# Convolution attention's score products from 16-bit halves instead of 32-bit operands, on one Trainium2 core

## The reference

```
k, v, q = conv1x1(x, wk, bk), conv1x1(x, wv, bv), conv1x1(x, wq, bq)   # (4, 128, 1024) each
attn    = softmax(einsum('bcn,bcm->bnm', v, q), axis=2)                # (4, 1024, 1024)
av      = einsum('bcn,bnm->bcm', k, attn)                              # (4, 128, 1024)
x       = relu(bn2(conv1x1(bn1(wwg @ av), wout, bout)) + x)
t       = tokens(x);  t = t + attention_8_heads(layernorm(t));  t = t + moe_8_experts_top2(layernorm(t))
```

## Time and profile before

| | |
|---|---|
| Three runs, median | 1309.75 us (1306.08 to 1310.2) |
| Profiled execution, its own time | 1310.52 us |
| Its span, first to last instruction | 1308.7 us (1.8 us lie around it) |
| TensorE busy | 88% of the span |
| VectorE busy | 61% |
| ScalarE busy | 48% |
| GpSimd busy | 44% |
| Mean granted TensorE clock | 0.936 of full speed |

### The profile page before, as it was taken

How to read it: one execution, slowest core, us unless ns; L and a number is a source line. 1 busy time by engine, 2 the same in 40 slices (tenths; PEclk the granted TensorE clock), 3 DMA queues, 4 the chain that set the end, 5 groups by cost and what they waited for, 6 DMA issues and landing times. The chain is left out here.

```text
span 1308.7 us, 29280 instructions
## 1 busy us (share of the span) xinstructions
PE 1151.3 (88%) x10343; PEld 759.2 (58%) x10343; DVE 792.5 (61%) x1425; ACT 630.8 (48%) x1129; POOL 577.6 (44%) x455
## 2 busy tenths in 40 slices
PE   3999799996589999999999998159999999999993
PEld 2555454644334444445445444049999999998772
DVE  2546545565578878778877871735565556555540
ACT  0636356464257756775776675223333333333332
POOL 1314224241358865276257526434444444444330
PEclk9989899896679999999999999569999999999996
DMA  4126652443412323232142413712333323332227
GB/s 125 50 65 208 272 168 88 139 144 110 129 41 55 79 77 73 73 97 90 43 110 78 106 43 100 269 34 41 49 50 49 51 49 50 49 50 43 41 32 263
DMA packets 99246, 120.47 MB, mean 92 GB/s; under 512 B 29400, under 2 KB 76440, under 8 KB 98488
## 3 DMA queue, kind: packets, MB, share of 16 engines
q1 hardware_dynamic: 78152, 70.29, 18.3%
q0 software_dynamic: 20544, 42.22, 14.5%
q10 hardware_dynamic: 432, 6.29, 1.2%
HBM read 72.97 MB, written 45.60 MB: 91 GB/s over the span
## 5 line engine op out<-in xcount | busy, mean ns | idle before, releaser
L823 ACT ACTIVATE WB<-PP 128x512 f32<-128x512 f32 x512 | 268.5, 606 | 167.5 <-PE PP L1132 167.4
L1449 DVE TENSOR_REDUCE mxp<-PP 128x2 f32<-128x1024 f32 x256 | 301.3, 1218 | 66.4 <-PE PP L1065 65.1
L868 ACT ACTIVATE WORK<-PP,b1c 128x256 f32<-128x256 f32 (+1 forms) x320 | 143.5, 449 | 258.4 <-PE PP L896 254.8
L633 POOL TENSOR_TENSOR WB<-WB 128x1024 f32<-128x1024 f32 x80 | 188.6, 2358 | 79.5 <-PE PP L1121 71.3
L896 PE MATMUL PP<-WORK,WB 128*128 128x256 f16 (+1 forms) x1920 | 207.9, 264 | 3.2 <-DVE WORK L1750 3.1
L1244 PE MATMUL PP<-WB,WORK 128*128 x1704 | 193.8, 273 | 0.0
L896 PEld LDWEIGHTS PP<-WORK,WB 128*128 x1920 | 176.6, 99 | 29.6 <-issue 4.2
L1244 PEld LDWEIGHTS PP<-WB,WORK 128*128 128x128 f16 x1704 | 164.4, 98 | 20.9 <-issue 0.4
L1132 PE MATMUL PP<-WORK 97*128 97x256 f16 x1024 | 160.6, 281 | 8.5 <-ACT WB L823 5.4
L601 POOL TENSOR_TENSOR WB<-WORK,WB 128x1024 f16<-128x1024 f32 x32 | 68.1, 2129 | 218.4 <-ACT WORK L734 218.4
L697 POOL DMA_INDIRECT res_d<-WORK,lb x71 | 115.7, 1630 | 102.8 <-DVE WORK L1777 87.5
(11 more groups left out here) (255 smaller groups left out, 1169.4 us busy)
## 6 DMA issues: line engine op xcount, KB each, us to landing
WORK<-in_L_ffn_W_dram POOLq DMA_DIRECT2D x32, 512.0 KB, 4.3
res_d<-WORK SPq DMA_DIRECT2D x8, 1024.0 KB, 4.5
late_d<-WB POOLq DMA_DIRECT2D x1, 6144.0 KB, 18.7
WB<-late_d ACTq DMA_DIRECT2D x3, 2048.0 KB, 17.8
WORK<-in_x_dram SPq DMA_DIRECT2D x8, 512.0 KB, 3.8
v_d<-WORK SPq DMA_DIRECT2D x4, 1024.0 KB, 4.8
WORK<-q_hi_d SPq DMA_DIRECT2D x16, 256.0 KB, 3.9
WORK<-v_d SPq DMA_DIRECT2D x8, 512.0 KB, 5.6
```

Of the source, the lines that this page charges most:

```text
L633: pool.tensor_tensor(PS[n % 2], PR[n % 3][:, 0], PR[n % 3][:, 1], ALU.add).then_inc(s("pair_kept"), 1)
L823: act.activation(PR[n % 3][:, c // 2, c % 2 * 2:c % 2 * 2 + 2], SCORES[m % 3] .rearrange("p (h n) -> p h n", h=2), ACT.Exp).then_inc(s("e_ ...
L868: act.activation(hid[u][:, k, 0:width], hidden_bank(k)[:, 0:width], ACT.Gelu, bias=b1c[:, bass.ds(e, 1), k], scale=1.0 / WSCALE)\
L1449: dve.tensor_reduce(mxp[:, n // 4 % 2, i, h:h + 2, k], PP[2 + h // 2][:, :].rearrange("p (h n) -> p h n", h=2), X_AXIS, ALU.max).then_inc( ...
```

## The change

Queries and values of the convolution attention are no longer kept as f32. Each is kept as two f16 tensors in the same bytes: the value rounded to f16 (index 0), and what that rounding left, again in f16 (index 1). ScalarE writes the first (same instruction, f16 output). VectorE writes the second in one new instruction each for q and v, `low_halves`: PSUM plus bias minus the first half. It stands at the head of `keep_k`, so ahead of the write of k on VectorE. Each score product of 512 columns becomes three f16 matmuls summed in the same bank: lead with lead, lead of v with rest of q, rest of v with lead of q. The product of the two rests is left out. TensorE waits for `q_low` and `v_low` in place of `q_kept` and `v_kept`, in both places. Two semaphore names that nothing used make room for the new two.

```
-        q_sb, v_sb = QV[:, 0:N], QV[:, N:2 * N]
+        qc, vc = [QV[:, i * N:(i + 1) * N].bitcast(F16).rearrange("p (s n) -> p s n", s=2) for i in range(2)]
...
             def keep_q(n):
                 act.wait_ge(s("q_made"), n + 1)
-                act.activation(q_sb, PP[0][:, :], ACT.Identity, bias=vec[:, BQ:BQ + 1]).then_inc(s("q_kept"), 1)
+                act.activation(qc[:, 0], PP[0][:, :], ACT.Identity, bias=vec[:, BQ:BQ + 1]).then_inc(s("q_kept"), 1)
...
             def keep_v(n):
                 act.wait_ge(s("v_made"), n + 1)
-                act.activation(v_sb, PP[1][:, :], ACT.Identity, bias=vec[:, BV:BV + 1]).then_inc(s("v_kept"), 1)
+                act.activation(vc[:, 0], PP[1][:, :], ACT.Identity, bias=vec[:, BV:BV + 1]).then_inc(s("v_kept"), 1)
...
                 def scores(i):
                     if i == 0:
-                        pe.wait_ge(s("q_kept"), b + 1)
-                        pe.wait_ge(s("v_kept"), b + 1)
+                        pe.wait_ge(s("q_low"), b + 1)
+                        pe.wait_ge(s("v_low"), b + 1)
...
                     for h in range(2):
                         product(PP[i % 3][:, h * HALF:(h + 1) * HALF],
-                                [(v_sb[:, i * P:(i + 1) * P], q_sb[:, h * HALF:(h + 1) * HALF])],
+                                [(vc[:, sv, i * P:(i + 1) * P], qc[:, sq, h * HALF:(h + 1) * HALF])
+                                 for sv, sq in ((0, 0), (0, 1), (1, 0))],
                                 "sc_made" if h else None)
...
                 if not last:
                     project_x(b + 1, False)
-                    pe.wait_ge(s("q_kept"), b + 2)
-                    pe.wait_ge(s("v_kept"), b + 2)
+                    pe.wait_ge(s("q_low"), b + 2)
+                    pe.wait_ge(s("v_low"), b + 2)
...
+            def low_halves(n):
+                for made, to, at, name in ((PP[0], qc, BQ, "q"), (PP[1], vc, BV, "v")):
+                    dve.wait_ge(s(f"{name}_kept"), n + 1)
+                    dve.scalar_tensor_tensor(out=to[:, 1], in0=made[:, :], scalar=vec[:, at:at + 1], in1=to[:, 0],
+                                             op0=ALU.add, op1=ALU.subtract).then_inc(s(f"{name}_low"), 1)
+
             def keep_k(n):
+                low_halves(n)
                 dve.wait_ge(s("k_made"), n + 1)
```

More of the change, by code:

```diff
@@ L297, in s @@
             return S[name]
-        for name in ("ld_w ld_x0 ld_x1 x_used pool_const pe_prep dve_prep act_prep mv_prep "
+        for name in ("ld_w ld_x0 ld_x1 x_used pool_const pe_prep dve_prep act_prep q_low "
                      "q_made v_made k_made q_kept v_kept k_kept sc_made max_kept exp_kept ks_kept "
@@ L303, in hybrid_block @@
                      "vt_kept_a vt_kept_v res0_kept st_res0 st_v st_q0 st_q1 "
-                     "ld_stage0 ld_stage1 scaled split_hi split_lo st_last wts_split "
+                     "ld_stage0 ld_stage1 v_low split_hi split_lo st_last wts_split "
                      "ld_g0 ld_g1 ld_m0 ld_m1 sum_kept rin_kept rstd_kept ld_nm mx_made mx_kept pair_kept ld_sum inv_kept st_inv ld_inv0 ld_inv1 st_made e_kept pv_made nrm_kept "
```

## The result

The changed kernel took 1293.62 us (median of 4 runs, 1290.95 to 1294.65) against 1309.28 us for the kernel before (4 runs, 1306.08 to 1310.2): ratio 0.9879, 95% interval 0.9866 to 0.9893, so 15.7 us less.

The account below looks back on a forecast made before the run. TensorE was taken to bound the score loops: 13.5 us from the products, less 1.2 (scores 3), 1.4 (keys 6) and 0.3 (store), gives 10.6, so 1309.75 becomes 1299 us. Range 1294 to 1305.

Parts of the forecast that it names:

- The products: Score loops on TensorE: three f16 matmuls at 0.216 us replace 0.86 us of f32, saving 13.5 us in all.
- The wait before scores 3: Head of the score loop: TensorE waits for exponential 0 on ScalarE, since they share a bank; 0.3 us lost a pass.
- The collision on keys 6: Score loop: VectorE's scaling for tile 6 waits out a GpSimd instruction, delaying weigh 6 by 0 to 0.7 us a pass; 0.35 taken.
- The rests: Two more VectorE instructions a pass, before k, lie in idle time with 1.0 us in hand; cost taken 0.
- The store: Pass 1: a 6 MB store delays the next image's x load; up to 0.3 us of the gain stays behind.
- another chain in the loop: Rival: in the score loop late keys 6 or the staging ring take over from TensorE; 1302 to 1305, chance 0.13.
- uncovered rests: Rival: VectorE's rests run slower or start late before the transposes; up to 5.1 us lost, 1304, chance 0.06.
- no effect: Rival: in the score products, f16 records at 0.29 us make three as dear as two f32 ones; 1309, chance 0.05.
- a slower run: Rival: granted clock falls in the score loops; a third of each at the lower level gives 1330, chance 0.05.
- overlapping matmuls: Rival: a score bank's three products overlap wholly and the ring bounds the loop; 6 us less a pass, 1286, chance 0.01.
- The clock dip: Score loops: granted clock falls, work takes twice its time; gain gone from 3 us of such work a pass, chance 0.05.
- The sustained figure of 131 ns: Skill's pace for 512-column matmuls in a stream; would put a product at 0.39 us and the products' gain at 30 us.

Follow-up runs that it names:

- e3: Changed kernel with a fourth product, rest with rest, for each score bank: 1313.2 us against 1316.53 for the kernel before, 0.9981.
- e9: Kernel before with the fourth weight part moved out of the score loop, after exponential 7: 1313.11 us against 1309.18 for the kernel before, 1.0022.
- e2: Kernel before, f32 products kept, plus the two VectorE rest instructions a pass and TensorE's waits on them: 1315.42 us against 1316.53, 0.9991.
- e8: Changed kernel with v's rest made three times before TensorE is told: 1302.74 us against 1309.18 for the kernel before, 0.9947.
- e10: Changed kernel with the 6 MB store cut in three 2 MB stores started earlier: 1289.61 us against 1310.39 for the kernel before, 0.9834.
- e11: Kernel before with the 6 MB store cut in the same three 2 MB stores: 1302.24 us against 1310.39 for the kernel before, 0.9937.
- e4: Changed kernel with two products for each score bank, without the queries' rests: 1299.77 us against 1316.53 for the kernel before, 0.9877.
- e6: Changed kernel with one product for each score bank, lead by lead: 1290.32 us against 1310.39 for the kernel before, 0.9852.
- the other three sets: Changed kernel, no edit, run again three times against the kernel before: ratios 0.9908, 0.9873 and 0.9885.
- e1: Changed kernel run again, no edit: 1304.2 us against 1316.53 for the kernel before, 0.9908.

## Why the prediction was wrong in size

- **The products**: right. 0.216 us a matmul was measured, 0.42 us a tile, 13.5 us, and e3 shows that inside the loop nothing but the pace counts.
- **The wait before scores 3**: mis-sized. 0.3 us a pass was taken off. The four tiles of scores 0 to 3 take 189.19 - 183.87 = 5.32 us for 24 matmuls at 0.216, 5.18 us, so 0.14 are lost, all of it before scores 3, and another 0.03 before the second weigh. The kernel before had lost 0.07 that the changed one does not: 198.79 - 191.85 = 6.94 for 6.87, and there the first f32 record alone is followed 0.50 us later in place of 0.43. So 0.1 a pass on balance, not 0.3. The forecast had counted these 0.07 into the distance from a block's end to its maximum (0.27; without them 0.20, and 0.19 in the changed kernel), so exponential 0 was done at 3.95 us, not 4.03.
- **The collision on keys 6**: the step that failed. The forecast took 0.35 us a pass for it and said that today's collision costs nothing. It costs 0.2 us a pass in the kernel before (e9): keys 6 end at 215.94 us and weigh 6 starts 0.15 behind them, at 216.09, where the pace would have had it at 215.96; the forecast saw TensorE still at weigh 5 when keys 6 were done, and left out this handover. In the changed kernel it costs 0.6 us in one of 24 loops and nothing in the other 23. The timeline of before had it in plain sight, three weighs in 5.35 us; I read idle brackets and not starts. So a loss of 1.4 us was in truth a gain of about 0.8 in most runs. That the forecast couldn't tell who starts first was fair, since 0.05 us decide it; the half that it took was a guess.
- Both together: 13.5 + 0.8 - 0.4 = 13.9, where the forecast had 10.6 and the loops measured 14.0, or 13.4 with one collision.
- **The rests**: right, cost 0 (e2), cover 0.84 us (e8) for 1.0.
- **The store**: named, and small as forecast for the change itself (waits for x of 5.4, 5.2, 7.4 and 7.5 us in four traces of the changed kernel against 5.96 and 5.8 before). What it is worth by itself, 5 to 8 us (e10, e11), I did not ask.
- **The rivals**: another chain in the loop was right in kind and wrong in place (e4: with two products the head of the loop waits for exponential 0; only with one, in e6, do late keys hold TensorE up); uncovered rests, no effect, a slower run and overlapping matmuls all fell. The clock dip is real in e6 only. The sustained figure of 131 ns for 512 columns (the Trainium skill, TensorE: Matmul & The Clock Gate, section Back-to-back issue gap) has no support here: 0.216 us in every f16 stream of the loops and of the earlier trace rows.
- **The range**: it began at 13.5 plus 2 us, but the first set gave 15.7. With the collision counted on the right side, the most to be had was 14.3 and the range would have begun near 1293.5. No rival had a gain above 13.5 beside the overlap of matmuls, which fell. Which side of its edge the time falls on is partly luck: with the ratios of the other three sets, 1309.75 would become 1297.7, 1293.1 and 1294.7. The mean of four sets, 14.9, stands some 1 us above the loops' 13.4 to 14.0. That is open, but for the 0.35 us of the last pass that come with the rests (e2). Two candidates: the low-clock time, which varies from 150 to 167 us by trace; and the last transposes of the kernel, which spread over 11.3 us in all four traces of the changed kernel and 11.3 to 11.4 in e3, e6 and e8, and over 12.4 to 12.6 in all five with f32 products, though over 12.3 in e4 and 13.3 in e10. No run separates them, and the sets' own spread (12.3 to 15.9) is larger than the question.

## What to carry to other kernels

Three f16 matmuls in place of one f32 matmul save a quarter of its TensorE time, and they pass on all of it where TensorE fills the loop and the rests are made in another engine's idle time. Before taking off for a new wait, check whether the old kernel already pays it: compare starts of blocks with the pace times their number, since short waits don't show as idle (an f32 record here is 0.59 us long at a pace of 0.43, so the first 0.16 us of a wait stay hidden under it). A single set of runs can be off by 2 us here while 23 of 24 loops repeat to 0.03 us; for a gain of one per cent, read the loop.

## What the runs showed of the hardware

- A scaling of 0.28 us on VectorE took 2.26 us when it met a GpSimd instruction of 2.13 us whose record starts 0.05 us behind its own, and ended 0.08 us after it. In the 23 other loops with three products the same two, 0.05 to 0.07 us apart, took 0.29 us and 2.20 to 2.23:

```profile
270.54 2.26 DVE L1376 TENSOR_SCALAR WORK<-WORK,rinv 128x128 f32<-128x128 f32 x1
...
270.59 2.13 POOL L601 TENSOR_TENSOR WB<-WORK,WB 128x1024 f16<-128x1024 f32 x1 [1.39 <-ACT WORK L734]
```

- The granted clock fell to its lower level after idle pieces of 1.84 to 2.19 us in all four loops of e6, and did not after 0.83 to 1.00 us (e4) nor after 2.03 us in one place of e1. The length of the piece alone does not decide.
- A 6 MB store started by GpSimd held back 0.5 MB loads of another queue: in the kernel before it ran from 138.3 to 156.9 us, and the two x loads started at 149.8 and 153.6 landed at 159.3 and 160.7, 9.5 and 7.1 us later, where the others took 3.5 to 4.5. TensorE stood 5 to 9 us for them in the traces with this store, and 0.24 with the same bytes in three stores begun earlier.
- In all 20 loops with f32 scores the first record of the loop was followed 0.50 to 0.51 us later, the others 0.43. With f16 scores the first was followed after the same 0.215 us as the rest.
